# Order of K, P.V and the block sends in turns 0 and 1 of a gated cross-attention kernel

## What is computed

```python
h_q = (rmsnorm(layernorm(x)) * ln_weight) @ w_q.T      # 32 heads of 128
h_k, h_v = ctx @ w_k.T, ctx @ w_v.T
score = einsum("bqhd,bkhd->bhqk", h_q, h_k) + position_bias[None]
score = softmax(where(m, score, -inf))
attn = einsum("bhqk,bkhd->bqhd", where(m, score, 0), h_v)
x = x + tanh(g_xattn) * (layernorm(x) + attn @ w_out.T)
x = x + tanh(g_ffn) * experts(layernorm(x))            # top 2 of 28, rank 8
```

## Time and profile before

| | us |
|---|---|
| three runs | 848.27, 848.75, 848.85 (median 848.75) |
| the profiled execution | 850.35 |
| its span, first to last instruction | 848.6 |
| PE busy | 821.9 (97%) |
| DVE, ACT, POOL busy | 594.8, 380.5, 442.6 |
| mean granted TensorE clock | 0.991 |

### The profile page before, as it was taken

How to read it: one execution, slowest core, us unless ns; L and a number is a source line. 1 busy time by engine, 2 the same in 40 slices (tenths; PEclk the granted TensorE clock), 3 DMA queues, 4 the chain that set the end, 5 groups by cost and what they waited for, 6 DMA issues and landing times.

```text
span 848.6 us, 14325 instructions
## 1 busy us (share of the span) xinstructions
PE 821.9 (97%) x4270; PEld 702.8 (83%) x4270; DVE 594.8 (70%) x999; ACT 380.5 (45%) x1046; POOL 442.6 (52%) x406
## 2 busy tenths in 40 slices
PE   8979999999999999969999999999999999998998
PEld 6868888877788889858888888888888888887886
DVE  6886555767736354747887779777887788779852
ACT  5554444443433424443456344644555345642410
POOL 1365666676475473547545764477446754571200
PEclk9999999999999999969999999999999999999999
DMA  8228444543635554665665456555655566544001
GB/s 305 93 81 272 166 161 149 174 161 99 199 110 189 174 198 156 216 219 156 220 220 183 155 204 223 203 150 190 239 197 180 172 220 221 191 159 154 1 25 74
DMA packets 78556, 145.48 MB, mean 171 GB/s; under 512 B 7872, under 2 KB 44736, under 8 KB 76608
## 3 DMA queue, kind: packets, MB, share of 16 engines
q1 hardware_dynamic: 78528, 145.12, 50.7%
HBM read 94.77 MB, written 50.33 MB: 171 GB/s over the span
## 4 chain that ended last, share of the span: by engine, by line
PE 84%; DVE 6%; DMA 3%; issue 2%; POOL 2%; ACT 2%; SPq 1%; DVEq 0%; POOLq 0%; ACTq 0%
PE proj_ps L1810 16%; PE proj_ps L1618 13%; PE proj_ps L1866 12%; PE proj_ps L1885 7%; PE score_ps L1618 7%; PE proj_ps L1686 4%; PE score_ps L1885 4%; PE score_ps L1655 3%; PE proj_ps L2051 3%; PE turn_ps L1866 2%; PE pv_ps L1866 2%; PE pv_ps L1885 2%; PE turn_ps L1885 2%; PE score_ps L1686 2%; PE turn_ps L1655 2%
## 5 line engine op out<-in xcount | busy, mean ns | idle before, releaser
L574 POOL TENSOR_TENSOR comb<-mask_add,bias_sb 128x1024 f32<-128x1024 f32 x32 | 77.3, 2438 | 163.7 <-DVE attn L1380 163.7
L778 ACT ACTIVATE attn<-attn,neg_max 128x128 f32<-128x128 f32 x256 | 99.2, 391 | 34.9 <-DVE neg_max L1369 34.9
L984 ACT ACTIVATE w_hi<-w_raw 128x256 fp32r<-128x256 f32 x105 | 39.8, 413 | 102.9 <-POOL w_raw L648 70.0
L1402 DVE TENSOR_TENSOR acc<-proj_ps,acc 128x512 f32<-128x512 f32 x70 | 48.3, 689 | 37.3 <-PE proj_ps L1618 37.3
L658 POOL TENSOR_TENSOR w_lo<-w_raw,w_hi 128x256 fp32r<-128x256 f32 x105 | 73.4, 742 | 0.0
L610 POOL TENSOR_TENSOR w_lo<-w_raw,w_hi 128x256 fp32r<-128x256 f32 x60 | 47.4, 796 | 27.2 <-ACT w_hi L849 27.2
L1618 PE MATMUL proj_ps<-w_hi,tf_hi 128*128 128x512 f32 x156 | 61.1, 392 | 0.4 <-DVE tf_lo L1398 0.4
L1618 PE MATMUL proj_ps<-w_lo,tf_hi 128*128 128x512 f32 x156 | 60.7, 389 | 0.0
L1618 PE MATMUL proj_ps<-w_hi,tf_lo 128*128 128x512 f32 x156 | 60.7, 389 | 0.0
L1264 DVE TENSOR_TENSOR w_lo<-w_raw,w_hi 128x1024 fp32r<-128x1024 f32 (+1 forms) x20 | 28.2, 1426 | 41.0 <-ACT w_hi L884 41.0
L884 ACT ACTIVATE w_hi<-w_raw 128x1024 fp32r<-128x1024 f32 (+1 forms) x28 | 27.6, 1014 | 57.3 <-POOL w_raw L694 21.3
(11 more groups left out here) (326 smaller groups left out, 2542.4 us busy)
## 6 DMA issues: line engine op xcount, KB each, us to landing
w_raw<-in_weights SPq DMA_DIRECT2D x52, 512.0 KB, 5.5
v_sb<-v_spill SPq DMA_DIRECT2D x32, 512.0 KB, 3.7
q_spill<-attn SPq DMA_DIRECT2D x60, 256.0 KB, 3.0
qt<-q_spill SPq DMA_DIRECT2D x15, 1024.0 KB, 4.8
block_spill<-block_sb SPq DMA_DIRECT2D x30, 512.0 KB, 3.5
attn<-block_spill SPq DMA_DIRECT2D x120, 128.0 KB, 2.9
w_raw<-in_v_weights SPq DMA_DIRECT2D x12, 512.0 KB, 4.8
v_spill<-v_sb SPq DMA_DIRECT2D x12, 512.0 KB, 4.6
```

Of the source, the lines that this page charges most:

```text
L574: pool.tensor_tensor(comb[:, j, :, :], mask_add[:, :, :], bias_sb[:, j:j + 1, :].to_broadcast([P, B, S]), ALU.add).then_inc(comb_done, 1)
L778: e = act.activation(probs[:, u, i, :], probs[:, u, i, :], ACT.Exp, bias=neg_max[:, u, i:i + 1], accum_out=row_sum[:, u, i:i + 1])
L1402: dve.tensor_tensor(acc[:, b, :], out_banks[b][:, :], acc[:, b, :], ALU.add).then_inc(acc_done, 1)
```

## The change

On PE, `values(0)` moves behind the first five products of `k_stage(1)`; three of its groups stand there, and the fourth after the sixth product. For this the P.V groups of turn 0 get other banks, and `k_stage(1)` loses its `at_split` waits. Turn 1 is written out on PE, ACT and DVE; the loops begin with turn 2. On SP the load of K's weights for pair 2 (`refill_k(0)`) moves from behind the last `fetch_blocks(0)` to behind `load_bias(1)`, and `send_blocks(0, 1)` moves ahead of `load_v(0, 0)` and `fetch_blocks(0, 0)`. On POOL the four sums of K's weights (`ks_forms(1)`) move ahead of `add_mask(1)`, and `add_mask(1)` no longer waits for the four `normalise` of turn 0 (`probs_done`), but only for the four bias additions (`biased`). SP's loop of turns is as it was.

```diff
--- before.py
+++ after.py
@@ -210,7 +210,9 @@
 
             if isinstance(a, int) and a == LAST:
                 return (pv_ps, score_ps[0], score_ps[1], pv_ps)[u]
-            if isinstance(a, int) and a in (0, LAST - 1) and u == 0:
+            if isinstance(a, int) and a == 0:
+                return (proj_ps[3], score_ps[0], score_ps[1], turn_ps)[u]
+            if isinstance(a, int) and a == LAST - 1 and u == 0:
                 return proj_ps[3]
             return pv_banks[u]
 
@@ -470,6 +472,7 @@
 
             last = VG - 1
             load_bias(1)
+            refill_k(0)
             for s in q_stored.values():
                 sp.wait_ge(s, 16 * NQ)
             load_q(1)
@@ -481,16 +484,15 @@
             send_blocks(0, 0)
             sp.wait_ge(v_post, last * VPOSTS + 16)
             store_v(last, "21b", v_11, 1, 0, 1)
-            sp.wait_ge(v_stored["22"], 32 * VG)
-            fetch_blocks(0, 0)
+            send_blocks(0, 1)
             sp.wait_ge(v0_stored, 16)
             sp.wait_ge(v_stored["21a"], 16 * VG)
             load_v(0, 0)
-            send_blocks(0, 1)
+            sp.wait_ge(v_stored["22"], 32 * VG)
+            fetch_blocks(0, 0)
             sp.wait_ge(v_stored["21b"], 16 * VG)
             load_v(0, 1)
             fetch_blocks(0, 1)
-            refill_k(0)
             for n in ("11", "12"):
                 sp.wait_ge(v_stored[n], 32 * VG)
 
@@ -724,10 +726,16 @@
                 v_second_sums(g)
             k_forms(0)
             v_last_sums(VG - 1)
-            pool.wait_ge(probs_done, UNITS)
+            ks_forms(1)
             add_mask(1)
+            rest_ka(1, 1, 0, 0, 0)
+            rest_ks(1, 2, 0)
+            rest_ka(1, 3, 2, 1, 1)
+            rest_ks(1, 4, 1)
             k_last_sum(0)
-            k_forms(1)
+            rest_ks(1, 5, 2)
+            rest_ka(1, 6, 1, 0, 1)
+            rest_ks(1, 7, 3)
             rest(WO, 0)
             with pool.Fori(1, LAST - 1) as a:
 
@@ -1014,19 +1022,10 @@
             def iteration(a):
                 exps(a, 0)
                 exps(a, 1)
-                if isinstance(a, int) and a == 0:
-                    exps(a, 2)
-                    exps(a, 3)
-                    k_copy(a, 1, s_copy, k1_ps)
-
-                    act.wait_ge(v_post, VG * VPOSTS)
-                    act.wait_ge(v_last, VG * VTILES)
-                    k_copy(a, 2, k_w, k5_ps)
-                else:
-                    k_copy(a, 1, s_copy, k1_ps)
-                    exps(a, 2)
-                    k_copy(a, 2, k_w, k5_ps)
-                    exps(a, 3)
+                k_copy(a, 1, s_copy, k1_ps)
+                exps(a, 2)
+                k_copy(a, 2, k_w, k5_ps)
+                exps(a, 3)
                 k_copy(a, 6, k_at(0), k1_ps)
 
             def attention(a):
@@ -1034,13 +1033,44 @@
                     lead_at(a, u)
 
             lead_k(0)
-            iteration(0)
-            act.wait_ge(v_prod, VG * VFORMS * VTILES)
+            for u in range(UNITS):
+                exps(0, u)
+            k_copy(0, 1, s_copy, k1_ps)
+            act.wait_ge(w_in[WK], 48)
+            lead_ka(1, 0, 0, 0)
+
+            act.wait_ge(v_post, VG * VPOSTS)
+            act.wait_ge(v_last, VG * VTILES)
+            k_copy(0, 2, k_w, k5_ps)
+            lead_ks(1, 0)
+            act.wait_ge(k_prod, 3)
+            lead_ka(1, 2, 1, 1)
+            act.wait_ge(k_prod, 4)
+            lead_ks(1, 1)
+            act.wait_ge(k_prod, 5)
+            lead_ks(1, 2)
+            k_copy(0, 6, k_at(0), k1_ps)
+            lead_ka(1, 1, 0, 1)
+            act.wait_ge(k_prod, PRODUCTS)
+            lead_ks(1, 3)
+            exps(1, 0)
             lead(WO, 0)
+            exps(1, 1)
+            k_copy(1, 1, s_copy, k1_ps)
+            exps(1, 2)
+            k_copy(1, 2, k_w, k5_ps)
+            exps(1, 3)
+            lead_at(0, 0)
+            lead_at(0, 1)
+            lead_at(0, 2)
+            k_copy(1, 6, k_at(0), k1_ps)
+            lead_at(0, 3)
             lead(WV, 1)
-            lead_k(1)
-            attention(0)
-            with act.Fori(1, LAST - 1) as a:
+            lead_k(2)
+            act.wait_ge(out_done, B)
+            lead(WO, 1)
+            attention(1)
+            with act.Fori(2, LAST - 1) as a:
                 iteration(a)
                 lead_k(a + 1)
 
@@ -1401,19 +1431,22 @@
                 dve.wait_ge(out_done, a * B + (b + 1))
                 dve.tensor_tensor(acc[:, b, :], out_banks[b][:, :], acc[:, b, :], ALU.add).then_inc(acc_done, 1)
 
+            def k_add(i, n, dst, ps, add):
+                dve.wait_ge(k_prod, i * PRODUCTS + n)
+                dve.tensor_tensor(dst, ps[:, :], add, ALU.add).then_inc(k_post, 1)
+
+            def k_first_posts(i):
+
+                dve.wait_ge(k_copied, i * COPIES + 1)
+                k_add(i, 4, k_t, k6_ps, s_copy)
+                dve.wait_ge(k_post, i * KPOSTS + 1)
+                k_add(i, 5, k_v, k7_ps, k_t)
+                dve.wait_ge(k_post, i * KPOSTS + 2)
+                k_add(i, 3, kt[:, 1, half(0)], k4_ps, k_v)
+
             def k_posts(i):
-
-                def post(n, dst, ps, add):
-                    dve.wait_ge(k_prod, i * PRODUCTS + n)
-                    dve.tensor_tensor(dst, ps[:, :], add, ALU.add).then_inc(k_post, 1)
-
-                dve.wait_ge(k_copied, i * COPIES + 1)
-                post(4, k_t, k6_ps, s_copy)
-                dve.wait_ge(k_post, i * KPOSTS + 1)
-                post(5, k_v, k7_ps, k_t)
-                dve.wait_ge(k_post, i * KPOSTS + 2)
-                post(3, kt[:, 1, half(0)], k4_ps, k_v)
-                post(7, kt[:, 0, half(1)], k5_ps, k_t)
+                k_first_posts(i)
+                k_add(i, 7, kt[:, 0, half(1)], k5_ps, k_t)
 
             def iteration(a):
                 for u in range(UNITS):
@@ -1451,8 +1484,26 @@
                 k_posts(0)
 
             first_iteration()
-            attention(0)
-            with dve.Fori(1, LAST - 1) as a:
+            for u in range(UNITS):
+                add_bias(1, u)
+            normalise(1, 0)
+            normalise(1, 1)
+            dve.wait_ge(block_out[0], 16)
+            turn_probs(1, 0)
+            k_first_posts(1)
+            rest_at(0, 0)
+            rest_at(0, 1)
+            normalise(1, 2)
+            rest_at(0, 2)
+            normalise(1, 3)
+            dve.wait_ge(block_out[1], 16)
+            turn_probs(1, 1)
+            k_add(1, 7, kt[:, 0, half(1)], k5_ps, k_t)
+            rest_at(0, 3)
+            for b in range(B):
+                add_out(0, b)
+            attention(1)
+            with dve.Fori(2, LAST - 1) as a:
                 iteration(a)
                 attention(a)
 
@@ -1674,7 +1725,7 @@
                     pe.wait_ge(block_in[t], a * (16 * NB) + 16 * NB)
                     if isinstance(a, int) and a == 0:
 
-                        pe.wait_ge(*((v_post, VG * VPOSTS), (k_copied, COPIES), (k_post, KPOSTS), (k_post, KPOSTS - 1))[u])
+                        pe.wait_ge(*((v_post, VG * VPOSTS), (biased, UNITS + 3), (biased, UNITS + 4), (k_post, KPOSTS + 1))[u])
                     elif isinstance(a, int) and a == LAST - 1 and u == 0:
 
                         pe.wait_ge(acc_done, a * B + 7)
@@ -1690,6 +1741,8 @@
             def out_proj(a, b):
 
                 pe.wait_ge(at_split, a * UNITS - (HP if b < BU else 0))
+                if isinstance(a, int) and a == 1 and b == 2:
+                    pe.wait_ge(at_split, UNITS - 1)
                 if b in (1, 2):
 
                     pe.wait_ge(biased, a * UNITS + (b + 2))
@@ -1922,13 +1975,13 @@
             for g in range(VG):
                 v_group(g)
 
-            def k_stage(a):
+            def k_stage(a, between=None):
                 i = a
 
                 def bank_free(n):
                     if isinstance(a, int) and a == 0:
                         pe.wait_ge(v_post, (VG - 1) * VPOSTS + 12 + n)
-                    else:
+                    elif not (isinstance(a, int) and a == 1):
                         pe.wait_ge(at_split, (a - 1) * UNITS + (n + 1))
 
                 bank_free(1)
@@ -1946,9 +1999,13 @@
                 pe.wait_ge(biased, a * UNITS + 2)
                 pe.wait_ge(k_lo, i * PRODUCTS + 5)
                 k_product(k7_ps, KS3, KT3)
+                if between:
+                    between(0)
                 pe.wait_ge(k_lo, i * PRODUCTS + 6)
                 pe.wait_ge(k_copied, i * COPIES + 1)
                 k_product(k1_ps, KA12, KB21, False)
+                if between:
+                    between(1)
                 pe.wait_ge(k_lo, i * PRODUCTS + 7)
                 pe.wait_ge(k_copied, i * COPIES + 2)
                 k_product(k5_ps, KS4, KB22, False)
@@ -1976,10 +2033,17 @@
                 for u in range(UNITS):
                     pv(a, u)
 
+            def first_values(place):
+                for u in ((0, 1, 2), (3,))[place]:
+                    pv(0, u)
+
             k_stage(0)
             all_scores(1)
```

(7 more changed lines are left out.)

## The result

The changed kernel is **slower**: 854.8 us (853.6 to 856.1, 4 runs) against 848.51 (848.25 to 848.85, 4 runs), ratio 1.0061 [1.0046, 1.0076]. The forecast was 845.4, and the range ended at 850.0. So the difference is about half a per cent, clear of the noise, and the forecast had the other sign. The profiled execution had a span of 854.3, 5.7 more than that of before.

A forecast was written before the change was run, and what follows sets the result against it. PE, busy 97% of the span, was taken as the bound, so time falls only where it waits or runs slow. -13.9 + 4.4 + 6.2 = -3.3 from 848.75 gave 845.4, range 840.8 to 850.0.

The forecast's parts named there:

- What the change takes away: At the seam around pair 1's scores and P.V of pair 0: 13.9 lost to waits, clock and matmul ends come back.
- New wait 1: Ahead of pair 1's scores: POOL's `add_mask(1)` collides with DVE's `normalise`, so PE begins them 4.4 later.
- New wait 2: In P.V of turn 1 (`values(1)`): blocks come late behind SP's queue, 2.6 ahead and 3.6 in the middle, 6.2.
- The clock: In the two new waits: a fall of PE's clock was charged 0 in the sum and left to a rival.
- Rival 1: PE's clock falls in one new wait (848.3, chance 0.26) or in both (851.2, chance 0.07).
- Rivals 2 and 3: No POOL/DVE collision in `normalise`: 841.0, chance 0.12; turn 1's block exchange in time but for 1.0: 840.3, chance 0.06.
- Rival 4: POOL one instruction further ahead; PE waits at K's second product of turn 0 and at the scores: 852.1, chance 0.08.

The follow-up runs named there:

- E3: Changed kernel with `add_mask(1)` waiting for `normalise` again and turn 1's Q, weights and first block send ahead of V on SP: 842.12, ratio 0.9900 to the kernel before.
- E7: The kernel of E3 run again, beside the changed kernel in one job: 840.98, ratio 0.9885 to the kernel before.
- E10: The kernel before with only 12 filling identity products on PE, meant for the idle stretch at 57.3 to 60.7: 847.61, ratio 0.9975 to the kernel before.
- E1: Changed kernel with `add_mask(1)` again after `normalise`, one low part of K's weights ahead, K's last sum ahead of three others: 849.83, ratio 0.9987 to the kernel before.
- E4: The kernel before with the wait for the four `normalise` ahead of `add_mask(1)` left out: 853.47, ratio 1.0040 to the kernel before.
- E5: The changed kernel itself, run again beside later experiments: 854.46, ratio 1.0045 to the kernel before.
- E6: Changed kernel with filling identity products: 12 ahead of pair 1's scores, 12 ahead of P.V of turn 1, 6 in its middle: 852.61, ratio 1.0023 to the kernel before.
- E9: E6 with 22 filling products ahead of P.V of turn 1 and 14 in its middle: 852.41, ratio 1.0031 to the kernel before.
- E8: E7 with 12 filling products early in the program, which came out at 48.8: 838.63, ratio 0.9854 to the kernel before.
- E2: Changed kernel with turn 1's Q, two weights and first block send issued on SP ahead of V: 846.89, ratio 0.9954 to the kernel before.

## Why the prediction was wrong

- **What the change takes away (-13.9): right in its places, and the size is that of one execution.** K's weights are issued at 342.83 (forecast 340.4) and GpSimd's first sum starts at 346.63 (344.4), with no wait behind it. The three waits are gone. E3 and E7, without the two new waits, come out 8.9 and 9.4 under before by their medians. E3's profiled execution, the fastest, is 12.6 under that of before (837.78 and 850.35). E7's has 1.6 of wait left in P.V of turn 1 and the fall of the clock at 61 us, 1.3; so part of what is missing to 13.9 is again the blocks of turn 1. Another part is not there in every execution: E10's profile of the same seam loses 12.1 (13.9 - 44.9 + 43.1), because the clock came back sooner. (Two readings of rows were off and change little: the clock of before was back at 379.8, not 379.6, and the row at 361.39 names V's load, so it shows only that the first blocks were there by then.)
- **New wait 1 (+4.4): right in place, cause and size,** 4.7 by rows: 0.77 ahead of K's last product and 3.32 ahead of the scores, where 0.9 and 3.5 were forecast, and 0.6 in starts after waits. E1 takes it away, and E4 puts the collision into the kernel before by leaving out one line. The rule of the Trainium skill (page "SBUF — State Buffer", section "SBUF: two separate sides"), that the two exclude each other for the whole instruction, agrees with the trace: 1.92 and 2.85 for instructions of 0.16 and 0.69.
- **New wait 2 (+6.2): right in place and cause, and too small. This is the first step that failed.** I took 2 MB in 5.3 for the queue's pace "since the queue's rows are of the same four transfers", and left the full queue's 243 GB/s as a bound, "5 more". From the start of P.V's last group to the second half of the blocks I had 0.9 + 20.0; the profiles of the changed kernel, E5 and E1 show 22.4, 23.8 and 24.5, and E6 and E9 show 25.9 and 25.2, of which 1.5 and 2.0 lie beside the code packets. Value and bound are 20.9 and 25.9, so the truth was about halfway. The term is then 7.7, 9.1 and 9.8 in the first three profiles, and with it and full clock the sum is -13.9 + 4.7 + 7.7 to 9.8 = -1.5 to +0.6: the two new waits took back most or all of what the change takes away, even without the clock. In E9, where the clock was held, the term is 10.3 and the sum +1.1, or -0.9 if the late second send was the fill's own.
- **The clock (0): the second.** Rival 1 with both falls (0.07) is what happened. An idle stretch of 3.32 behind one of 0.77 took the clock away, and so did one of 3.45. The first cost 2.6, where 2.9 was worked out. At the second, half clock lay on both halves of P.V, up to 405.94. The first half's loss was in the shadow of the second blocks; the second half's, 1.8, was not. In E5's profile the clock was back in time and this part is 0, so it too comes and goes. I had multiplied one price by two falls and not asked what ends the stretch behind each.
- The two together, by the rows of the changed kernel's profile: -3.3 + 0.3 (wait 1) + 2.6 + 1.5 + 1.8 = +2.9, and 5.2 - 2.3 = 2.9 is what the rows show for turn 2. In this profile the clock's part (2.6 + 1.8) is larger than that of the queue (1.5); in E5's they are about even (2.6 and 2.9).
- **Ahead of all that, 2.3 in the profile** were not in the sum: 1.0 at the start of the program and 1.3 at 61 us, where the clock fell after the idle stretch of 3.42 that the prediction had as its example of a clock that stays. In ten profiles with that stretch (before, changed, E1 to E7, E9) it fell in seven; in the two with 1.5 (E8, E10) it stayed. Reading one profile, I took for a property of 3.4 us what was a throw. E10 gains 2.0 in the kernel before, so the fall doesn't belong to the change.
- **The chances.** I gave 0.33 to rival 1. The rows had one stretch of 3.56 with a fall and one of 3.4 without. Both new waits were forecast at just that length, and the clock's terms were nearly as large as the whole gain of 3.3. That asked for a forecast with the falls in it. The page "TensorE: Matmul & The Clock Gate", section "HAM oscillation", of the Trainium skill warned of short bursts between DMA waits, and the trace agrees at the second place, 0.50 after the wait of 3.45 for the blocks; the wait of the first fall was for VectorE. What the falls cost by the rows did not come back in full: filled idle time gave 1.9 (E6) and 1.2 (E9) by the ratios, hardly clear of the noise, because the blocks came later.
- Rivals 2 and 3 did not come. Their conditions had to be built, as E1 and E2, and even then the ratios were 0.9987 and 0.9954, not the 0.991 and 0.990 of 841.0 and 840.3, for in each the other new wait and its fall of the clock were left or grew, and the sums had them too small. Rival 4's place came in E4, in the kernel before.

## What to carry to other kernels

A wait that is removed hands its time to the next late thing, so price the transfers of the next turn between the fastest and the slowest row of a full queue, and let the slowest decide where the range ends. Before an edit lets GpSimd start earlier, look at what VectorE does at that microsecond with two SBUF operands. And a clock that stayed up in one profile after an idle stretch of 3.4 us is one throw: put its fall into the sum, but ask at each place whether the engine or a transfer ends the stretch behind it.

## What the runs showed of the hardware beyond what I expected

- Idle TensorE time can be filled with products of no use, and the clock stays at 1.00 (E6 at 357 to 364, E9 at 388 to 404), while the transfers or VectorE set the end as before.
- Work put ahead of an idle stretch does the same when it shortens it: 3.42 to 1.53, for 2.0 to 2.4 us in two kernels (E10, E8). The fall itself had cost 1.3 in the changed kernel's profile; the rest is not explained.
- With the clock held, the blocks of turn 1 gained little: TensorE was 4.8 to 5.4 us earlier at P.V of turn 0 than in the changed kernel's profile (E9, E6), and only 1.8 to 2.0 at the second blocks. What makes the same 3 MB slower in one execution than in another (8.9 to 10.9 from send to fetch) was not tried and stays open.
- Code is loaded over the DMA engines as well, in packets of 16 KB, and in the two kernels with matmuls added at this place one of them lies in the exchange of blocks (E6 at 394.72, E9 at 391.74). Beside it the exchange was 1.5 and 2.0 longer. Whether it was the cause is open.
